# Four transformer layers on one core: another order inside the steps of the second layer, and a split, transposed output projection in the last

## The chip, the cores and the metric

The kernel runs on one core of a Trainium2 chip. The metric is the device time of one execution in microseconds (us), lower is better.

## The reference, cut to what matters

Four layers work one after the other on a residual x of 16 x 256 tokens by 128 features, all in float32. Each normalizes x and adds an attention branch and a feed-forward branch. The second and the last layer are the ones that matter here.

```
# second layer: 16 heads of 64, sequences of 256, sparse causal mask; 8 experts of 256, the best two gate
xn = layernorm(x)
x  = x + attention(xn) @ w_out + sum_e square(relu((xn * gate_e) @ up_e.T)) @ down_e.T
# gate_e = sigmoid(xn @ gate_w.T)[e] where e is among the two largest of sigmoid + expert_bias, else 0

# last layer: 16 heads of 64, causal mask; the linear feed-forward is one 128x128 matrix and a bias
xn = layernorm(x)
x  = x + softmax(q k^T / 8 + mask) v @ Wo + bo + xn @ (int4(kernel) + a @ b) + bias
```

## The kernel before, in words

Every engine has its own program, written out by hand, and the engines meet only at counting semaphores. The second layer (`second_layer`, lines 1119 to 1586) and the last layer (`last_layer`, from line 2052) are built alike. The work is cut into 8 passes of 512 tokens (two sequences), and each pass into 8 pairs of heads: 64 pairs, `N` in the code. A loop over steps `s` runs over the pairs as a software pipeline. In step s, TensorE (PE in the profile) does, in program order:

1. the scores of pair s-1 (L1250 and L1253 in the second layer, L2136 and L2139 in the last), 
2. the weighted values of pair s-3 (L1265, L1269; L2151, L2155),
3. four `turned` units of pair s-2, transposes of the softmax weights (L1278; L2164), with the query projection of pair s between the second and the third (L1230 to L1232; L2116 to L2118), 
4. the key projection of pair s, by the same lines,
5. `output` of pair s-3: the output projection of the pair, summed over the pass in one PSUM bank, `ACC` (L1286; L2172 and L2175),
6. in the second layer: the first up projection of expert (s-2) mod 8 (`up`, L1295 to L1297), `down` of pair s-3 (L1303), and the second up projection,
7. in some steps one more item (below),
8. `values` for step s+1 (L1239 to L1241; L2125 to L2127).

The projections in float32r (fp32r) are three products of a high and a low part: hi x hi, lo x hi, hi x lo; one float32r instruction is one record of the trace. A plain float32 product shows as two records.

The last item of a step in the second layer depends on s mod 8. At 6 it is `turn`, which transposes the normalized rows of the next pass (L1210). At 7 it is `logits`, ahead of the key projection (L1217). At 0 it is `gates_turned` (L1223). At 3, from step 11 on, it is `turned_back` (L1311), which transposes the finished sum of a pass back to rows.

**Two PSUM banks, `RING`, serve all these items in turn.** The list `ITEMS` gives their order. An item may be written when the item two places before it has been read: `ring` in `pe_` waits for it, through `taken`. Who reads what: ScalarE (ACT) copies queries, keys, values and `turn`; VectorE (DVE) multiplies an up projection with its gate (`gated`, L1494) and adds `turned_back` to x (`added`, L1500). In the list before, the two up projections stand side by side and `values` is last.

VectorE's order in a step of the second layer: the four `maxima` of pair s-1 (L1476, L1477; two instructions and their accumulator reads each), the four copies `turned_out` of pair s-2 (L1486) with two reciprocals among them (`sums`, L1481), the first `gated`, then one part of the next pass's normalization (s mod 8 = 4 `moments`, 5 `normed`, 6 `rest` (L1454), 7 `gates`, which is nine dependent instructions, L1460 to L1470), the second `gated`, and `added` at 3. `turned` on TensorE waits for `maxima` of the next pair, because both use the same banks. `rest` waits for ScalarE's two copies of `turn` (L1383, L1384). GpSimd (POOL) scales the weights (L1550) and squares the gated values (L1556), which `down` reads.

In the last layer `output` multiplies in plain float32 with the heads' output as stationary operand: four products of 128 columns per pair (L2175), and once a pass four more with the folded feed-forward matrix (L2172). `ACC` then holds rows, and `added` (L2303) adds it in two halves to x; each half is stored by its own DMA (L2367). ScalarE's `heads_out` (L2215) brings the heads' output from PSUM to SBUF. VectorE's order is that of the second layer without `gated` (maxima L2286 and L2287, copies L2296, reciprocals L2291), GpSimd's only the scaling (L2348).

Of the kernel before, what the change touches and what calls it, by code (L numbers as in the profile page):

```python
# [11 lines left out]
PASSES = B // 2  # L12
# [70 lines left out]
def program(nc, ins, out):  # L83
# [3 lines left out]
    with ctx:  # L87
# [1031 lines left out]
        def second_layer():  # L1119
# [28 lines left out]
            for s in range(-1, N + 4):  # L1148
# [6 lines left out]
                if 0 <= s - 2 < N:  # L1155
                    ITEMS += [("u", 2 * (s - 2)), ("u", 2 * (s - 2) + 1)]
# [30 lines left out]
            ended.update(r_full=r_full, r_taken=r_act, xs_s=xs_s, dv=dv, s_f=s_f, s_mx=s_mx, s_ex=s_ex, s_rc=s_rc, s_nm=s_nm, s_t=s_t, s_te=s_te,  # L1187
# [11 lines left out]
            def pe_(pe):  # L1199
# [120 lines left out]
                for s in range(-1, N + 4):  # L1320
# [107 lines left out]
            def dve_(dve):  # L1428
# [77 lines left out]
                for s in range(-1, N + 4):  # L1506
# [17 lines left out]
                    if 0 < i < PASSES:  # L1524
# [527 lines left out]
        def last_layer():  # L2052
# [14 lines left out]
            ot = [carve(512) for _ in range(2)]  # L2067
# [10 lines left out]
            for s in range(-1, N):  # L2078
                if s >= 0:
                    ITEMS += [("q", s), ("k", s)]  # L2080
                if (s + 2) % PAIRS == 0 and s + 2 < N:
                    ITEMS.append(("t", (s + 2) // PAIRS))
                if s + 1 < N:
                    ITEMS.append(("v", s + 1))
            item = {what: n for n, what in enumerate(ITEMS)}

# [10 lines left out]
            ln_b = sem("l3_biased")  # L2097

            def pe_(pe):
                def ring(kind, n):  # L2100
                    past(pe, r_taken, item[kind, n] - 1)
# [27 lines left out]
                def scores(g):  # L2129
                    past(pe, r_taken, item["k", g] + 1)  # L2130
# [11 lines left out]
                def weighted(g):  # L2142
                    i, j = divmod(g, PAIRS)
                    past(pe, s_te, UNITS * (g + 1))
                    past(pe, r_taken, item["v", i * PAIRS + j // 4 * 4 + 3] + 1)
                    past(pe, s_ot, g)
# [36 lines left out]
                for s in range(-1, N + 3):  # L2183
                    if 0 <= s - 1 < N:
                        scores(s - 1)
                    if 0 <= s - 3:
# [11 lines left out]
                    if 0 <= s - 3:  # L2198
                        output(s - 3)
                    if ("t", (s + 2) // PAIRS) in item and s >= 0 and (s + 2) % PAIRS == 0:  # L2200
                        turn((s + 2) // PAIRS)
                    if s + 1 < N:
                        values(s + 1)

            def act_(act):
# [6 lines left out]
                def heads_out(g):  # L2212
                    past(act, s_pv, g + 1)
                    past(act, o_f, g - 1)
                    act.activation(ot[g % 2], HEADS_OUT[:, :], ACT.Copy).then_inc(s_ot.s, 1)  # L2215
# [17 lines left out]

                turned_out(0)
                for s in range(-1, N + 3):
# [263 lines left out]
```

## Time and profile before

| | us |
|---|---|
| median of 3 runs | 2066.94 (2066.08 to 2068.91) |
| the profiled execution | 2069.05 |
| its span | 2067.2 |
| TensorE busy in the span | 1877.5 (91%) |
| VectorE, ScalarE, GpSimd busy | 1324.3, 1125.2, 869.7 |
| mean granted TensorE clock | 0.959 of full |
| second layer's steps | about 422 to 1154 |
| last layer's steps | about 1576 to 2067 |

Times in the trace count from the span's start. An engine's busy time includes all its instructions that compute; matmuls overlap at their ends, so a step is best measured from one start to the next. The row of an instruction says how long its engine stood idle before it, and for whom, in square brackets; no bracket means that nothing of note was waited for.

### The profile page before, as it was taken

The numbers are of one execution on the slowest core, as the hardware profiler recorded it, in microseconds if no ns is written. First come the engines' busy times: TensorE is split into PE (matmuls) and PEld (weight loads), VectorE is DVE, ScalarE is ACT, GpSimd is POOL, SyncE is SP. The second block draws the span as 40 slices with busy tenths as digits, with TensorE's granted clock in tenths as the row PEclk, the third lists the DMA queues.
The fourth block names the chain that finished last, engine by engine and source line by source line (L and its number), as shares of the span: only waits on it lengthen the run. The fifth ranks groups of instructions, "written<-read, shape, count | busy, mean of one in ns | idle before, by whom it ended". The sixth has DMA issues, their size and how long they took to land.

```text
span 2067.2 us, 40179 instructions
## 1 busy us (share of the span) xinstructions
PE 1877.5 (91%) x13354; PEld 1339.7 (65%) x13354; DVE 1324.3 (64%) x4752; ACT 1125.2 (54%) x3357; POOL 869.7 (42%) x1361
## 2 busy tenths in 40 slices
PE   5787888389999999999999899999998999999999
PEld 2555654266666666666666566666666777777777
DVE  6999973365656565665565566666653666766665
ACT  3444253154545455555555356555555777777776
POOL 4112266545544545454545311111112555555554
PEclk9899699689999999999999899999998999999999
DMA  6000016631010201011010000000000000000000
GB/s 195 22 2 1 2 34 153 130 133 37 7 42 1 42 1 42 6 37 42 1 42 1 1 1 1 1 1 1 1 1 1 7 1 7 7 7 7 6 7 6
DMA packets 74970, 53.62 MB, mean 26 GB/s; under 512 B 7056, under 2 KB 72976, under 8 KB 73872
## 3 DMA queue, kind: packets, MB, share of 16 engines
q1 hardware_dynamic: 69136, 46.73, 8.0%
q0 software_dynamic: 5632, 4.33, 1.5%
q8 instruction: 110, 1.80, 0.4%
q14 instruction: 92, 0.75, 0.1%
HBM read 40.30 MB, written 10.75 MB: 25 GB/s over the span
## 4 chain that ended last, share of the span: by engine, by line
PE 66%; DVE 9%; ACT 3%; issue 3%; POOL 1%; DMA 0%; POOLq 0%; DVEq 0%; ACTq 0%
PE bank L1303 5%; PE bank L1278 5%; PE bank L2164 4%; PE bank L1265 3%; PE bank L2151 3%; PE bank L1253 3%; PE bank L2175 3%; PE bank L1286 3%; PE bank L2139 3%; PE bank L1250 2%; PE bank L2136 2%; PE bank L1676 2%; PE bank L1747 2%; PE bank L1230 1%; PE bank L1297 1%
## 5 line engine op out<-in xcount | busy, mean ns | idle before, releaser
L1550 POOL TENSOR_TENSOR work<-work 128x128 f32<-128x128 f32 (+1 forms) x512 | 243.1, 506 | 248.1 <-DVE work L1481 248.0
L2348 POOL TENSOR_TENSOR work<-work 128x128 f32<-128x128 f32 (+1 forms) x512 | 243.2, 506 | 232.6 <-DVE work L2291 232.6
L1556 POOL TENSOR_TENSOR work<-work 128x512 f32<-128x512 f32 x128 | 133.0, 1040 | 109.5 <-PE bank L1303 61.1
L2296 DVE COPY work<-bank 128x384 f32<-128x384 f32 x256 | 134.5, 548 | 34.4 <-PE bank L2164 33.6
L1486 DVE COPY work<-bank 128x384 f32<-128x384 f32 x256 | 133.9, 547 | 34.4 <-PE bank L1278 34.4
L1379 ACT ACTIVATE work<-bank 128x512 f32<-128x512 f32 x64 | 38.2, 597 | 197.4 <-PE bank L1241 197.4
L1358 ACT ACTIVATE work<-work 128x128 f32<-128x128 f32 x256 | 100.6, 393 | 77.8 <-DVE work L1477 77.8
L2209 ACT ACTIVATE work<-work 128x128 f32<-128x128 f32 x256 | 100.5, 392 | 60.0 <-DVE work L2287 60.0
L2286 DVE CUSTOM_DVE_ANT_0 work<-bank,mask 128x128 f32<-128x128 f32 x256 | 73.5, 287 | 90.8 <-PE bank L2139 90.7
L1494 DVE SCALAR_TENSOR_TENSOR work<-bank,w_f 128x512 f32<-128x512 f32 x96 | 66.3, 690 | 95.3 <-PE bank L1297 95.3
L1359 ACT ACTIVATE work<-work 128x256 f32<-128x256 f32 x256 | 126.8, 495 | 0.0
L2210 ACT ACTIVATE work<-work 128x256 f32<-128x256 f32 x256 | 126.7, 495 | 0.0
L1303 PE MATMUL bank<-work,w_l 128*128 128x512 f32 x256 | 120.3, 592 | 0.0
L1476 DVE CUSTOM_DVE_ANT_0 work<-bank,mask 128x128 f32<-128x128 f32 x256 | 73.5, 287 | 72.2 <-PE bank L1253 71.8
L1278 PE MATMUL bank<-w_const,work 128*128 128x128 f32 x768 | 109.5, 278 | 0.4
L2164 PE MATMUL bank<-w_const,work 128*128 128x128 f32 x768 | 108.1, 277 | 0.0
L2287 DVE CUSTOM_DVE_ANT_0 work<-bank,mask 128x256 f32<-128x256 f32 x256 | 107.5, 420 | 0.0
L1477 DVE CUSTOM_DVE_ANT_0 work<-bank,mask 128x256 f32<-128x256 f32 x256 | 107.4, 420 | 0.0
L2031 POOL TENSOR_TENSOR work<-work,minus_half 128x4 f32<-128x4 f32 x8 | 8.5, 1060 | 227.7 <-DVEq L1893 227.7
L1278 PEld LDWEIGHTS bank<-w_const,work 128*128 128x128 f32 x768 | 86.8, 141 | 22.1 <-issue 13.6
L1295 PE MATMUL bank<-l_xn_hi,l_up_hi 128*128 128x512 f32 x128 | 99.7, 779 | 0.1
L2164 PEld LDWEIGHTS bank<-w_const,work 128*128 128x128 f32 x768 | 86.8, 141 | 20.1 <-issue 11.4
(389 smaller groups left out, 5436.3 us busy)
## 6 DMA issues: line engine op xcount, KB each, us to landing
w_f<-gates SPq DMA_DIRECT2D x48, 256.0 KB, 6.1
w_const<-gates SPq DMA_DIRECT2D x16, 256.0 KB, 5.7
w_l<-in_l SPq DMA_DIRECT2D x1, 3210.5 KB, 15.1
w_l<-in_l SPq DMA_DIRECT2D x2, 1540.0 KB, 7.5
w_f<-in_f SPq DMA_DIRECT2D x1, 3072.0 KB, 14.0
x_sb<-in_x SPq DMA_DIRECT2D x4, 512.0 KB, 5.8
normed_rows<-work SPq DMA_DIRECT2D x1, 2048.0 KB, 9.4
even_experts<-x_sb SPq DMA_DIRECT2D x8, 256.0 KB, 3.6
```

The costliest lines, as they stand in the source:

```text
L1278: mm = pe.transpose(PS[u][:, to * 128:(to + 1) * 128], pr[g % 2][u][:, c * 128:(c + 1) * 128], ident)
L1303: mm = pe.matmul(ACC[:, :], L["down"][:, (2 * e + c) * D:(2 * e + c + 1) * D], h2[c], start=False, stop=(e == PAIRS - 1 and c == 1), skip_ ...
L1359: act.activation(w[:, Q1], w[:, Q1], ACT.Exp, scale=-1.0, bias=nmx[:, g % 2, u, 1:2], accum_out=sm[:, g % 2, u, 1:2]).then_inc(s_ex.s, 1)
L1477: dve.tensor_tensor_reduce(w[:, Q1], PS[u][:, Q1], mask1[:, Q1], -1.0, BIG, ALU.add, ALU.min, nmx[:, g % 2, u, 1:2]).then_inc(s_mx.s, 1)
L1486: dve.tensor_copy(pt[u], PS[u][:, 0:384]).then_inc(s_te.s, 1)
L1550: ins_ = pool.tensor_tensor(w, w, spread(rc[:, g % 2, u, q:q + 1], w.shape[1]), ALU.mult)
L1556: pool.tensor_tensor(h2[u % 2], hs[u % 2], hs[u % 2], ALU.mult).then_inc(f_q.s, 1)
L2164: mm = pe.transpose(PS[u][:, to * 128:(to + 1) * 128], pr[g % 2][u][:, c * 128:(c + 1) * 128], ident)
L2210: act.activation(w[:, Q1], w[:, Q1], ACT.Exp, scale=-1.0, bias=nmx[:, g % 2, u, 1:2], accum_out=sm[:, g % 2, u, 1:2]).then_inc(s_ex.s, 1)
L2287: dve.tensor_tensor_reduce(w[:, Q1], PS[u][:, Q1], mask3[:, Q1], -1.0, BIG, ALU.add, ALU.min, nmx[:, g % 2, u, 1:2]).then_inc(s_mx.s, 1)
L2296: dve.tensor_copy(pt[u], PS[u][:, 0:384]).then_inc(s_te.s, 1)
L2348: ins_ = pool.tensor_tensor(w, w, spread(rc[:, g % 2, u, q:q + 1], w.shape[1]), ALU.mult)
```

## The change

In the second layer, TensorE's step ends differently. The item of step 7 (turn, gates_turned or turned_back) now stands right behind the first up projection, `down` behind it, then `values`, and the second up projection ends the step. `ITEMS` follows that order. On VectorE `added` moves ahead of the second `gated`, and `rest` and `gates` move behind it; `moments` and `normed` stay.

In the last layer the output projection is turned over and split: the weights are the stationary operand, the heads' output of 512 tokens is the moving one, and each is a high and a low float32r part. `ACC` now holds features by tokens, as in the second layer. So each pass is copied out by ScalarE, transposed back on TensorE as a ring item, and added in one piece; one step is added at the end. VectorE makes the low part of the heads' output (`heads_rest`) in every step. The parts of the weights are made once at the start.

```diff
 # second layer, ITEMS
-                    ITEMS += [("u", 2 * (s - 2)), ("u", 2 * (s - 2) + 1)]
+                    ITEMS.append(("u", 2 * (s - 2)))
...
                 if s + 1 < N:
                     ITEMS.append(("v", s + 1))
+                if 0 <= s - 2 < N:
+                    ITEMS.append(("u", 2 * (s - 2) + 1))
...
 # second layer, TensorE
                         up(2 * (s - 2))
-                    if 0 <= s - 3 < N:
-                        down(s - 3)
-                    if 0 <= s - 2 < N:
-                        up(2 * (s - 2) + 1)
...
                         turned_back((s - 11) // PAIRS)
+                    if 0 <= s - 3 < N:
+                        down(s - 3)
                     if s + 1 < N:
                         values(s + 1)
+                    if 0 <= s - 2 < N:
+                        up(2 * (s - 2) + 1)
...
 # second layer, VectorE
+                    if s >= 11 and (s - 11) % PAIRS == 0:
+                        added((s - 11) // PAIRS)
+                    if 0 <= s - 2 < N:
+                        gated(2 * (s - 2) + 1)
+                    if 0 < i < PASSES:
                         if at == 2:
                             rest(i)
                         if at == 3:
                             gates(i)
-                    if 0 <= s - 2 < N:
-                        gated(2 * (s - 2) + 1)
-                    if s >= 11 and (s - 11) % PAIRS == 0:
-                        added((s - 11) // PAIRS)
...
 # last layer, TensorE
                 def output(g):
                     i, j = divmod(g, PAIRS)
                     if j == 0:
-                        past(pe, o_e, 2 * i)
-                        for t in range(4):
-                            pe.matmul(ACC[:, t * 128:(t + 1) * 128], xnT[:, t * 128:(t + 1) * 128], w_eff, start=(t == 0), stop=False, skip_group_check=True)
-                    past(pe, s_ot, g + 1)
+                        past(pe, y_s, i)
+                        pe.matmul(ACC[:, :], w_eff, xnT, start=True, stop=False, skip_group_check=True)
+                    if g == 0:
+                        past(pe, w_lo, 1)
+                    past(pe, s_or, g + 1)
+                    ws = slice(j * 128, (j + 1) * 128)
+                    pe.matmul(ACC[:, :], wout_hi[:, ws], ot_hi[g % 2], start=False, stop=False, skip_group_check=True)
+                    pe.matmul(ACC[:, :], wout_hi[:, ws], ot_lo[g % 2], start=False, stop=False, skip_group_check=True)
+                    pe.matmul(ACC[:, :], wout_lo[:, ws], ot_hi[g % 2], start=False, stop=(j == PAIRS - 1), skip_group_check=True).then_inc(o_f.s, 1)
+
+                def turned_back(i):
+                    to = ring("b", i)
+                    past(pe, y_s, i + 1)
                     for t in range(4):
-                        mm = pe.matmul(ACC[:, t * 128:(t + 1) * 128], ot[g % 2][:, t * 128:(t + 1) * 128], L["wout"][:, j * 128:(j + 1) * 128],
-                                       start=False, stop=(j == PAIRS - 1), skip_group_check=True)
-                    mm.then_inc(o_f.s, 1)
+                        mm = pe.transpose(to[:, t * 128:(t + 1) * 128], yT[:, t * 128:(t + 1) * 128], ident)
+                    mm.then_inc(r_full.s, 1)
...
 # last layer, ScalarE: once at the start, and once a pass at s = 10, 18, ...
+                def sum_out(i):
+                    past(act, o_f, PAIRS * (i + 1))
+                    act.activation(yT, ACC[:, :], ACT.Copy).then_inc(y_s.s, 1)
...
+                act.activation(wout_hi, L["wout"], ACT.Copy).then_inc(w_hi.s, 1)
...
 # last layer, VectorE
+                def heads_rest(g):
+                    past(dve, s_ot, g + 1)
+                    past(dve, o_f, g - 1)
+                    dve.tensor_tensor(ot_lo[g % 2], HEADS_OUT[:, :], ot_hi[g % 2].bitcast(F32), ALU.subtract).then_inc(s_or.s, 1)
...
+                dve.tensor_tensor(wout_lo, L["wout"], wout_hi.bitcast(F32), ALU.subtract).then_inc(w_lo.s, 1)
...
-                        for u in (1, 2, 3):
+                        turned_out(s - 2, 1)
+                    if 0 <= s - 3 < N:
+                        heads_rest(s - 3)
+                    if 0 <= s - 2 < N:
+                        for u in (2, 3):
                             turned_out(s - 2, u)
```

## Rows read from the trace of the kernel before

**Rows 1.** Windows of the two layers: window, length, each engine's busy time, PEclk, DMA.

```profile
415.00:1140.00 725.00, 695.40 (x4218) 476.99 (x4218) 438.81 (x1705) 378.21 (x1314) 378.66 (x644) 0.98 0.12 31
1575.00:2067.00 492.00, 485.03 (x3988) 384.86 (x3986) 324.37 (x1522) 369.00 (x1293) 257.40 (x526) 1.00 0.02 6
```

**Rows 2.** TensorE's waits in the second layer: total us, times, longest.

```profile
PE bank L1239 <- DVE work L1494: 24.6, 21, 2.5
```

**Rows 3.** Timeline, start and length: first scores of steps 30 to 36.

```profile
743.35 0.49 PE L1250 MATMUL bank<-work 64*128 64x128 f32 x4
...
757.31 0.80 PE L1250 MATMUL bank<-work 64*128 64x128 f32 x4
...
770.03 0.49 PE L1250 MATMUL bank<-work 64*128 64x128 f32 x4
...
781.88 0.49 PE L1250 MATMUL bank<-work 64*128 64x128 f32 x4
...
792.38 0.49 PE L1250 MATMUL bank<-work 64*128 64x128 f32 x4
...
802.87 0.49 PE L1250 MATMUL bank<-work 64*128 64x128 f32 x4
...
814.42 0.49 PE L1250 MATMUL bank<-work 64*128 64x128 f32 x4
```

**Rows 4.** Timeline of all engines, end of step 30: turn, then rest on VectorE.

```profile
753.06 0.60 PE L1210 MATMUL bank<-w_const,work 128*128 128x128 f32 x4
...
754.81 0.69 DVE L1454 TENSOR_TENSOR l_xn_lo<-work,l_xn_hi 128x512 fp32r<-128x512 f32 x1 [3.27 <-ACT l_xn_hi L1384]
```

**Rows 5.** Windows behind the first pass's wait and behind the fourth's.

```profile
480.00:484.40 4.40, 2.71 (x23) 1.86 (x25) 2.16 (x9) 1.09 (x3) 1.04 (x1) 1.00 0.00 0
756.10:760.20 4.10, 4.04 (x21) 2.57 (x21) 1.20 (x9) 1.12 (x4) 1.04 (x1) 0.58 0.00 0
```

**Rows 6.** Timeline, end of step 34 and start of step 35, an undisturbed step.

```profile
802.28 0.69 DVE L1494 SCALAR_TENSOR_TENSOR work<-bank,w_f 128x512 f32<-128x512 f32 x1 [1.72 <-PE bank L1297]
...
802.55 0.40 PE L1241 MATMUL bank<-l_wv_hi,l_xn_lo 128*128 128x512 f32 x1
...
803.83 0.29 DVE L1476 CUSTOM_DVE_ANT_0 work<-bank,mask 128x128 f32<-128x128 f32 x1 [0.85 <-PE bank L1253]
...
806.78 0.40 PE L1231 MATMUL bank<-l_xn_lo,l_qk_hi 128*128 128x512 f32 x1
```

**Rows 7.** Timeline: gates of the first pass; gates in step 31 and what followed.

```profile
413.84 0.18 DVE L1460 TENSOR_SCALAR work<-work 128x32 f32<-128x32 f32 x1 [1.47 <-ACT work L1389]
...
417.07 1.88 DVE L982 TENSOR_TENSOR x_sb<-x_sb,w_f 128x1664 f32<-128x1664 f32 x1
...
767.64 0.17 DVE L1460 TENSOR_SCALAR work<-work 128x32 f32<-128x32 f32 x1
...
771.70 0.69 DVE L1494 SCALAR_TENSOR_TENSOR work<-bank,w_f 128x512 f32<-128x512 f32 x1
...
774.25 0.40 PE L1231 MATMUL bank<-l_xn_lo,l_qk_hi 128*128 128x512 f32 x1
```

**Rows 8.** Chain of waits in the last layer: start, length, line, records.

```profile
1801.32 0.44 PE bank L2108 x4
...
1815.45 0.23 PE bank L2118
1815.68 0.89 PE bank L2175 x8
```

**Rows 9.** VectorE's timeline in the same step of the last layer.

```profile
1814.69 1.02 DVE L2296 COPY work<-bank 128x384 f32<-128x384 f32 x2 [0.27 <-PE bank L2164]
1816.03 0.18 DVE L2291 RECIPROCAL work<-work 128x4 f32<-128x4 f32 x1 [0.32 <-ACT work L2210]
```

**Rows 10.** Timeline of all engines, end of the kernel.

```profile
2062.09 0.60 ACT L2215 ACTIVATE work<-bank 128x512 f32<-128x512 f32 x1 [3.44 <-PE bank L2155]
...
2063.93 0.75 DVE L2303 TENSOR_TENSOR x_sb<-x_sb,bank 128x256 f32<-128x256 f32 x2 [3.47 <-PE bank L2175]
```

More of the change, by code:

```diff
@@ L2066, in last_layer @@
             pt = [carve(384) for _ in range(UNITS)]
-            ot = [carve(512) for _ in range(2)]
+            ot_at = top[0]
+            carve(4, 512)
+            ot_hi, ot_lo = ([rounded(f"l3_{part}_{p}", "work", ot_at + (2 * n + p) * 512, 512) for p in range(2)]
+                            for n, part in enumerate(("heads_hi", "heads_lo")))
+            yT = carve(512)
+            wout_hi, wout_lo = rounded("l3_wout_hi", "w_l2", 0, WIDE), rounded("l3_wout_lo", "w_f0", WIDE, WIDE)
             nmx, sm, rc = carve(2, UNITS, 2), carve(2, UNITS, 2), carve(2, UNITS, 2)
@@ L2077, in last_layer @@
             ITEMS = [("t", 0)]
-            for s in range(-1, N):
-                if s >= 0:
+            for s in range(-1, N + 4):
+                if 0 <= s < N:
                     ITEMS += [("q", s), ("k", s)]
-                if (s + 2) % PAIRS == 0 and s + 2 < N:
+                if s >= 0 and (s + 2) % PAIRS == 0 and s + 2 < N:
                     ITEMS.append(("t", (s + 2) // PAIRS))
+                if s >= 11 and (s - 11) % PAIRS == 0:
+                    ITEMS.append(("b", (s - 11) // PAIRS))
                 if s + 1 < N:
@@ L2085, in last_layer @@
             item = {what: n for n, what in enumerate(ITEMS)}
+            by_act = [kind != "b" for kind, _ in ITEMS]
+            act_rank = [sum(by_act[:n]) for n in range(len(ITEMS))]
             def bank_of(kind, n):
@@ L2097, in last_layer, with taken @@
             ln_b = sem("l3_biased")
+            s_or, y_s = ended["f_d"].next(), ended["y_s"].next()
+            w_hi, w_lo = Count(g_bv, 3, 1), Count(g_sct, 1, 1)
+            def taken(eng, kind, n):
+                if kind == "b":
+                    past(eng, o_e, n + 1)
+                else:
+                    past(eng, r_taken, act_rank[item[kind, n]] + 1)
             def pe_(pe):
                 def ring(kind, n):
-                    past(pe, r_taken, item[kind, n] - 1)
+                    m = item[kind, n]
+                    if m >= 2:
+                        taken(pe, *ITEMS[m - 2])
                     return bank_of(kind, n)
@@ L2129, in scores @@
                 def scores(g):
-                    past(pe, r_taken, item["k", g] + 1)
+                    taken(pe, "k", g)
                     for p in range(2):
@@ L2182, in pe_ @@
                 pe.wait_ge(weights_rest, 3)
-                for s in range(-1, N + 3):
+                for s in range(-1, N + 4):
                     if 0 <= s - 1 < N:
                         scores(s - 1)
-                    if 0 <= s - 3:
+                    if 0 <= s - 3 < N:
                         weighted(s - 3)
@@ L2197, in pe_ @@
                         project("k", s)
-                    if 0 <= s - 3:
+                    if 0 <= s - 3 < N:
                         output(s - 3)
-                    if ("t", (s + 2) // PAIRS) in item and s >= 0 and (s + 2) % PAIRS == 0:
+                    if s >= 0 and (s + 2) % PAIRS == 0 and s + 2 < N:
                         turn((s + 2) // PAIRS)
+                    if s >= 11 and (s - 11) % PAIRS == 0:
+                        turned_back((s - 11) // PAIRS)
                     if s + 1 < N:
@@ L2248, in act_ @@
                         projected("k", s)
-                    if ("t", (s + 2) // PAIRS) in item and s >= 0 and (s + 2) % PAIRS == 0:
+                    if s >= 0 and (s + 2) % PAIRS == 0 and s + 2 < N:
                         turned_out((s + 2) // PAIRS)
+                    if s >= 10 and (s - 10) % PAIRS == 0:
+                        sum_out((s - 10) // PAIRS)
                     if s + 1 < N:
@@ L2278, in rest @@
                 def rest(i):
-                    past(dve, r_taken, item["t", i] + 1)
+                    taken(dve, "t", i)
                     dve.tensor_tensor(x_lo[i % 2], xnT, x_hi[i % 2].bitcast(F32), ALU.subtract).then_inc(xs_s.s, 1)
@@ L2308, in dve_ @@
                 rest(0)
-                for s in range(-1, N + 3):
+                past(dve, w_hi, 1)
+                dve.tensor_tensor(wout_lo, L["wout"], wout_hi.bitcast(F32), ALU.subtract).then_inc(w_lo.s, 1)
+                for s in range(-1, N + 4):
                     i, at = divmod(s + 4, PAIRS)
@@ L2329, in dve_ @@
                             rest(i)
-                    if s >= 3 and (s - 3) % PAIRS == PAIRS - 1:
-                        added((s - 3) // PAIRS)
+                    if s >= 11 and (s - 11) % PAIRS == 0:
+                        added((s - 11) // PAIRS)
             def pool_(pool):
@@ L2352, in pool_ @@
                 bias(0)
-                for s in range(-1, N + 3):
+                for s in range(-1, N + 4):
                     i, at = divmod(s + 4, PAIRS)
@@ L2364, in sp_ @@
             def sp_(sp):
-                for n in range(2 * PASSES):
-                    past(sp, o_e, n + 1)
-                    sp.dma_start(out_v[:, 2 * n:2 * n + 2, :], x_sb[:, 2 * n:2 * n + 2, :]).then_inc(stored, 16)
+                for i in range(PASSES):
+                    past(sp, o_e, i + 1)
+                    for n in (4 * i, 4 * i + 2):
+                        sp.dma_start(out_v[:, n:n + 2, :], x_sb[:, n:n + 2, :]).then_inc(stored, 16)
             pe_prog.append(pe_)
```

21 lines of the change are left out of this document (10 added, 11 removed).

## The prediction

> **What bounds the kernel now.** I read the page first: TensorE is busy for 91% of the span and no other engine for more than 64%. The windows of the two layers that change come next [rows 1]. In the second layer TensorE works 695.4 of 725 us, in the last 485.0 of 492, and the clock is full there. So in both layers a gain comes from less work on TensorE or from one of its few waits. The waits of TensorE in the second layer name one line: `values` (L1239) stands for 24.6 us in 21 places, 2.5 us at most, until VectorE has done a `gated` [rows 2]. The starts of the scores show where [rows 3]. An ordinary step is 792.38 - 781.88 = 10.50 us. Steps 30, 31, 32 and 35 (6, 7, 0 and 3 modulo 8) take 13.96, 12.72, 11.85 and 11.55. This pattern comes seven times.
>
> The timeline of step 30 tells why. `turn` starts at 753.06, ScalarE copies its result, and `rest` on VectorE can start only at 754.81, having waited 3.27 us [rows 4]. The second `gated` stands behind `rest` in VectorE's program, and `values` needs the bank that this `gated` reads. So TensorE's own transposes come back to it as a wait of 2.5 us. Behind the wait the clock is low: 0.58 of full over 4.10 us, against 1.00 behind the same wait of the first pass [rows 5]. A share of 0.58 is mostly the lower level of 1.2 GHz, and 4.10 x (1 - 0.58) = 1.7 us are lost by it, in steps 30 and 31.
>
> **Second layer, what goes.** In the new list the item of step 7 has the key projection two places before it, `values` has the first up projection, and the second up projection has the item. After `turn` come `down` (two float32 products as wide as the whole output projection, 0.89 each by [rows 8]) and `values` before the second up projection, over 2 us, and `turn` is read by two copies of ScalarE of 0.60 each (size as in [rows 10]). So steps 30 and 31 lose the wait and the slow clock: 2.5 + 1.7 = 4.2 us. In step 35 `turned_back` adds 11.55 - 10.50 = 1.05 us now, while four such transposes on the path of the last layer are worth 0.44 [rows 8]. `added` is done before the second up projection needs its bank, so 0.6 us go.
>
> **Second layer, what is late next.** In an ordinary step nothing changes. `gated` of the second up projection starts at 802.28 and the three float32r products of `values` took 3 x 0.23 = 0.70 us (size as L2118 in [rows 8]). With the two exchanged `gated` runs from 802.98 to 803.67, and `maxima` starts at 803.83, when the scores are there [rows 6]. That leaves 0.16 us. In step 30 `rest`, 0.69 us, now stands between them. `maxima` comes 0.5 to 0.6 us late.
>
> How much lateness of `maxima` TensorE bears is read from step 32. There `maxima` started at 771.70 + 0.6 = 772.3, which is 2.27 after the scores at 770.03, where 803.83 - 802.87 = 0.96 is usual: 1.3 late. The second query product stood at 774.25 - 770.03 = 4.22 after the scores, where 806.78 - 802.87 = 3.91 is usual: 0.3 late [rows 3, 6, 7]. So TensorE bears 1.0 us, `rest` costs nothing, and each further us of lateness is a us of waiting.
>
> `gates` is more than that. It now runs behind the second `gated`, directly ahead of `maxima` of step 32. Nine instructions took 771.70 - 767.64 = 4.06 us in step 31 and 417.07 - 413.84 = 3.23 in the first pass, where GpSimd was idle [rows 7]. Behind them on VectorE wait `maxima`, the copies and the reciprocals. For the first of these TensorE waits at its first `turned`, and ScalarE with all exponentials, from which heads, query and key copies hang. With 4.06 `maxima` starts 0.8 + 4.06 = 4.9 after the scores, 3.9 late, and TensorE stands 2.9 us. With 3.23 it is 2.1 us. I take 2.6, since GpSimd's square of the second up projection runs beside it at the new place too. ScalarE stays 1 us later than TensorE; `gates_turned` now needs the bank of the key copy directly behind the first up projection. This costs between 0 and 1.0; I take 0.4, as the up projection covers half. The clock costs between 0 and 1.7, as in [rows 5]. I take 0.9, since a part is hidden in the waits for ScalarE. The item itself is a transpose of one tile, 0.25 at most by the 0.44 for four. Step 32 is then 10.5 + 0.25 + 2.6 + 0.4 + 0.9 = 14.65, against 11.85: 2.8 us more.
>
> The Trainium skill, page "SBUF — State Buffer", section "SBUF: two separate sides", says that a VectorE instruction with two SBUF inputs and a GpSimd instruction that reads SBUF lock each other out for a whole instruction. By that rule only one square of about 1 us, begun some 0.5 us before, stands against `gates` at its new place, so it would take 3.7 us and TensorE would wait 2.5. The two durations in [rows 7] agree with such a lock.
>
> Per pass: -4.2 - 0.6 + 2.8 = -2.0 us. Seven times this is -14.0. In the first pass the clock had not fallen [rows 5], so 1.7 of it was never there: **second layer -12.3 us**. The ends are 0 + 1.7 + 7 x (-4.2 - 0.6 + 4.5) = about 0 and 7 x (-4.2 - 0.6 + 1.0) + 1.7 = -25. The DMAs of the gates start as late as before, since `gates_turned` comes some 2 us earlier in its step and the step 3 us later.
>
> **Last layer, per step.** The output projection of a pair is 0.89 us on the chain, and one float32r product of 128x512 is 0.23 [rows 8]. Three of them are 0.70: -0.19 us, and 64 pairs give -12.2. The four products with the feed-forward matrix become one of 512 columns, the same work, 0. New on TensorE are four transposes a pass, 0.44 each time [rows 8], seven of them inside: +3.1.
>
> The Trainium skill, page "FP8 and Floating Point Precision", section "TensorE Precision Notes", says that a true float32 product is four passes of the array. By that rule three passes in place of four would save 0.89 / 4 = 0.22 a pair, 14.2 in all.
>
> New on VectorE is `heads_rest`, 128x512 with one input in PSUM, 0.69 as `gated` [rows 6], between the second and the third copy. VectorE stands 0.27 before the third copy and 0.32 before the second reciprocal [rows 9], so 0.59 of it are covered and the reciprocal is at most 0.1 late. That feeds GpSimd's weights of the third and fourth unit, which TensorE wants in the next step. Cost 0; the lower end is a gain of 0 for the whole layer's steps, if the cover fails in part. ScalarE's `sum_out` (0.60) comes once a pass, where it waits for `values`. `wout_hi` and `wout_lo`, two instructions of 128x1024, run at the start and are wanted three steps later: 0. The waits of TensorE for `heads_rest` in place of ScalarE's copy are over a us before `output`.
>
> **Last layer, the end.** The last steps have no projections, and VectorE's copies are on the chain. `heads_rest` stands between them twice: +1.2. After the last ScalarE copy at 2062.09 to 2062.69 the sum was added from 2063.93 on, 1.24 later [rows 10]. Now come `heads_rest` 0.69, three products about 0.9, `sum_out` 0.60, four transposes 0.44 to 0.6, and about 0.05 at each of four hand-overs: 2.9, which is 1.7 more. The store of the first half no longer starts before the second half is added: +0.3. Together **+3.2**, between 1.5 and 4.5. The last layer: -12.2 + 3.1 + 3.2 = **-5.9 us**.
>
> **The sum.** -12.3 - 5.9 = -18.2. The profiled execution took 2069.05 (span 2067.2), so 2050.85. The median of the runs is 2066.94, 2.11 below it, which gives **2048.7**.
>
> **Rivals.**
> *The clock stays high.* If it does not fall behind the new wait of step 32, 0.9 x 7 = 6.3 go too: 2042.4. For it: in the first pass 2.5 us of waiting left the clock at 1.00, and the new wait is broken by the transposes of the first unit. Against it: the fourth pass [rows 5].
> *The wait only moves.* If TensorE stands 2.9, all of ScalarE's 1.0 and the whole 1.7 of clock are paid, step 32 is 4.5 longer, and the second layer gives about 0: 2066.94 - 5.9 = 2061. For it: `gates` needs 4.06 with GpSimd busy. Against it: waits for ScalarE and slow products overlap.
> *VectorE bounds the last layer, slower.* If `heads_rest` shifts the third and fourth copy so that its 0.69 stands on TensorE's path in each step, a step is 0.69 - 0.19 = 0.5 longer, 64 x 0.5 = +32. With +3.1 + 3.2 - 12.3 this is +26: 2093. It decides from the point where VectorE's idle time of 0.59 and the time until TensorE's next weighted values, in the next step, are used up. Against it: VectorE is busy for 324 of 492 us [rows 1], and 64 x 0.69 = 44 more are 75%.
> *The new order does nothing to the wait*, if `values` still waits for a `gated` behind `rest`. The program order excludes this.
>
> **Chances.** Forecast (gain of 9 to 24) 0.62; clock high 0.14; the wait only moves 0.14; slower by VectorE 0.05; other mishaps of either sign 0.05. Runs of this kernel differ by some 0.1%, so a change under 0.2% (4.1 us) can't be told from none. Faster by more than that 0.90, within it 0.04, slower 0.06. The range reaches from a high clock with short `gates` to most of the second rival: 2037 to 2060.
>
> **What would show it.** L1239 loses its waits for L1494. Steps 6, 7, 3 modulo 8 take about 10.95, 11.3 and 10.95; step 0 about 14.6, with TensorE standing at L1278's successor for VectorE's maxima behind `gates`. Steps of the last layer take 7.2 in place of 7.4. The forecast is wrong if step 0 stays at 12, or if a line of the last layer's transposes or weighted values begins to wait for VectorE in each step.

## The result, and the profile after

The changed kernel takes **2047.95 us** (median of four runs, 2046.20 to 2049.94). The kernel before took 2067.93 on the same chip (2066.08 to 2071.29). The ratio is 0.9902, with an interval of 0.9885 to 0.9919. The forecast was 2048.7, with 2037 to 2060 as its range.

The profiled execution took 2049.94 us with a span of 2048.1. The stages are those of [rows 1], but with both edges in the idle time beside the layers, and the two short windows are explained below. The columns are those of [rows 1].

```profile
410.00:1120.00 710.00, 682.04 (x4211) 471.88 (x4212) 437.64 (x1716) 377.23 (x1310) 378.86 (x636) 0.98 0.12 33
1560.00:2048.00 488.00, 476.07 (x3648) 361.21 (x3646) 357.07 (x1578) 373.06 (x1300) 257.56 (x526) 0.99 0.02 6
764.50:769.00 4.50, 2.33 (x28) 1.50 (x25) 4.22 (x16) 0.28 (x1) 1.04 (x1) 1.00 0.02 4
502.00:507.00 5.00, 5.00 (x19) 3.71 (x18) 2.53 (x8) 3.78 (x13) 3.42 (x8) 0.70 0.00 0
```

TensorE's waits in the second layer are the counterpart of [rows 2]. The line `values` had 24.6 us there. It is gone, and `turned` (L1280) waits for `maxima` (L1479) instead, once a pass. A short wait of `gates_turned` for ScalarE's copy is new too.

```profile
PE bank L1280 <- DVE work L1479: 15.2, 7, 2.2
...
PE bank L1225 <- ACT work L1375: 1.5, 5, 0.3
```

The first scores of steps 30 to 36 are the counterpart of [rows 3].

```profile
741.33 0.49 PE L1252 MATMUL bank<-work 64*128 64x128 f32 x4
...
752.26 0.49 PE L1252 MATMUL bank<-work 64*128 64x128 f32 x4
...
763.63 0.49 PE L1252 MATMUL bank<-work 64*128 64x128 f32 x4
...
777.15 0.49 PE L1252 MATMUL bank<-work 64*128 64x128 f32 x4
...
787.65 0.49 PE L1252 MATMUL bank<-work 64*128 64x128 f32 x4
...
798.13 0.49 PE L1252 MATMUL bank<-work 64*128 64x128 f32 x4
...
809.06 0.49 PE L1252 MATMUL bank<-work 64*128 64x128 f32 x4
```

From these starts and those of the other passes, a step measures as follows (s modulo 8; us; the mean over the passes where they differ):

| | before | after | forecast |
|---|---|---|---|
| second layer, ordinary step | 10.50 | 10.50 | same |
| step 6 | 13.90 | 10.93 | 10.95 |
| step 7 | 12.55 | 11.37 | 11.3 |
| step 0 | 11.84 | 13.81 (five of 13.53, one of 14.39, one of 14.63) | 14.65 |
| step 3 | 11.55 | 10.93 | 10.95 |
| **step 1's scores (the first) to step 63's** | 699.37 | 679.68: **-19.7** | -12.3 |
| last layer, ordinary step | 7.40 | 7.21 | 7.21 |
| step 6 / step 3 | 7.85 / 8.29 | 7.65 / 8.52 | |
| **step 1's scores (the first) to step 63's** | 467.97 | 459.42: **-8.6** | -9.1 |
| **step 63's scores to the span's end** | 23.08 | 28.9: **+5.8** | +3.2 |

Two parts outside these steps also moved. All that comes ahead of the second layer's first scores, where both kernels are the same, took 426.98 us after 422.62 (+4.4). In the traces of the experiments the same stretch took 422.46 to 435.64, so this is a spread between executions and chips. The stretch from step 63 of the second layer to the first scores of the last took 453.12 after 454.16 (-1.0). The sum is -19.7 - 8.6 + 5.8 + 4.4 - 1.0 = -19.1, the difference of the two spans. This is why the effects below are read from the lengths of steps, and the times only support them.

Step 32 starts at 763.63. These are VectorE, GpSimd and TensorE in it, from the timeline of all engines:

```profile
763.63 0.49 PE L1252 MATMUL bank<-work 64*128 64x128 f32 x4
763.74 0.69 DVE L1496 SCALAR_TENSOR_TENSOR work<-bank,w_f 128x512 f32<-128x512 f32 x1 [2.41 <-PE bank L1299]
...
764.35 0.17 DVE L1462 TENSOR_SCALAR work<-work 128x32 f32<-128x32 f32 x1
...
764.51 1.04 POOL L1559 TENSOR_TENSOR work<-work 128x512 f32<-128x512 f32 x1 [1.00 <-DVE work L1496]
...
764.94 0.66 DVE L1464 TENSOR_TENSOR work<-work,w_l 128x32 f32<-128x32 f32 x1
...
768.04 0.29 DVE L1478 CUSTOM_DVE_ANT_0 work<-bank,mask 128x128 f32<-128x128 f32 x1
...
768.83 1.08 PE L1280 MATMUL bank<-w_const,work 128*128 128x128 f32 x6 [2.17 <-DVE work L1479]
...
769.98 0.40 PE L1233 MATMUL bank<-l_xn_lo,l_qk_hi 128*128 128x512 f32 x1
```

`gates` runs from 764.35 to 768.04, which is 3.69 us. GpSimd's square stands beside it only once, and L1464 takes 0.66 there, where the same line takes 0.19 with GpSimd idle (the timeline of VectorE further below). TensorE waits 2.17 us. The lock-out that the Trainium skill tells of ("SBUF — State Buffer", section "SBUF: two separate sides") thus fits the rows. The estimates by it in the prediction, 3.7 for `gates` and 2.5 for the wait, lay nearer than the 2.6 that I took. They too are over the 2.17 of this row. The section on the prediction takes the same wait by the prediction's own measure.

The end of the kernel is the counterpart of [rows 10]:

```profile
2038.37 0.60 ACT L2248 ACTIVATE l_heads_hi<-bank 128x512 fp32r<-128x512 f32 x1 [4.04 <-PE bank L2178]
2039.00 0.69 DVE L2341 TENSOR_TENSOR l_heads_lo<-bank,l_heads_hi 128x512 fp32r<-128x512 f32 x1 [2.25 <-ACT l_heads_hi L2248]
...
2039.74 0.50 PE L2199 MATMUL bank<-l_heads_hi,l_wout_hi 128*128 128x512 f32 x1 [1.42 <-DVE l_heads_lo L2341]
...
2040.73 0.60 ACT L2269 ACTIVATE work<-bank 128x512 f32<-128x512 f32 x1 [1.77 <-PE bank L2201]
...
2041.47 1.09 PE L2207 MATMUL bank<-w_const,work 128*128 128x128 f32 x4 [0.78 <-ACT work L2269]
2042.60 0.69 DVE L2347 TENSOR_TENSOR x_sb<-x_sb,bank 128x512 f32<-128x512 f32 x1 [2.91 <-PE bank L2207]
2043.32 0.89 SPq L2417 DMA_DIRECT2D out_x<-x_sb  x2
```

From the end of the last copy of the heads to the end of the last add it is 2043.29 - 2038.97 = 4.32 us, against 1.99 before. The four transposes take 1.09 here.

### The profile page after: what moved, and what is told of

Same layout as the page of the kernel before. It is cut to its first block, busy times and chain, and to the rows that moved or that the text cites. A ratio compares the mean times of both kernels' runs of the same rounds, so it can differ in the third digit from the quotient of the medians.

```text
span 2048.1 us, 39644 instructions
## 1 busy us (share of the span) xinstructions
PE 1867.9 (91%) x13018; PEld 1317.7 (64%) x13018; DVE 1357.2 (66%) x4809; ACT 1130.1 (55%) x3366; POOL 873.2 (43%) x1361
## 4 chain that ended last, share of the span: by engine, by line
PE 63%; DVE 10%; ACT 4%; issue 3%; POOL 2%; DMA 0%; POOLq 0%; DVEq 0%; ACTq 0%
PE bank L1305 5%; PE bank L2187 4%; PE bank L1280 4%; PE bank L2174 3%; PE bank L1267 3%; PE bank L2162 3%; PE bank L1288 2%; PE bank L1255 2%; PE bank L2159 2%; PE bank L1252 2%; PE bank L1679 2%; PE bank L1750 2%; PE bank L2139 1%; PE bank L2140 1%; PE bank L2141 1%
## 5 line engine op out<-in xcount | busy, mean ns | idle before, releaser
L1280 PE MATMUL bank<-w_const,work 128*128 128x128 f32 x768 | 110.9, 281 | 15.4 <-DVE work L1479 15.2
L2326 DVE CUSTOM_DVE_ANT_0 work<-bank,mask 128x128 f32<-128x128 f32 x256 | 73.3, 287 | 74.3 <-PE bank L2162 74.2
L1280 PEld LDWEIGHTS bank<-w_const,work 128*128 128x128 f32 x768 | 88.3, 142 | 37.1 <-issue 28.8
L1479 DVE CUSTOM_DVE_ANT_0 work<-bank,mask 128x256 f32<-128x256 f32 x256 | 107.6, 420 | 0.0
L441 ACT ACTIVATE w_l<-bank 76x512 f32<-76x512 f32 x128 | 71.0, 590 | 51.0 <-PE bank L811 50.7
L323 POOL TENSOR_TENSOR w_l<-qk,w_const 128x304 f32<-128x304 f32 x16 | 12.0, 752 | 187.1 <-ACT qk L427 187.0
```

Source lines behind the costliest of these rows:

```text
L1280: mm = pe.transpose(PS[u][:, to * 128:(to + 1) * 128], pr[g % 2][u][:, c * 128:(c + 1) * 128], ident)
L1479: dve.tensor_tensor_reduce(w[:, Q1], PS[u][:, Q1], mask1[:, Q1], -1.0, BIG, ALU.add, ALU.min, nmx[:, g % 2, u, 1:2]).then_inc(s_mx.s, 1)
```

## The experiments

Each ran beside the kernel before on its chip. The first four shared one chip (before: 2069.02), as did the next four (2076.5) and the last two (2068.88). Ratios are against these. The times expected in experiments 5 to 8 were reckoned from kernels on a chip with 2068 to 2069, so there the steps and the ratios decide, not the microseconds.

**1. The second layer alone.** The changed kernel with the last layer of before, whole.

> The second layer of the changed kernel with the last layer of the kernel before: only the order of the second layer is changed. Theory (the two parts add up and the order is worth the most): the steps of the second layer sum to 19.7 us less, as in the trace after, so the time is about 17 to 20 us under the kernel before, near 2048 to 2050. Rival (part of the gain of the second layer in that trace is the state of the run, and the last layer gives more than its steps show): 10 to 13 us under it, near 2056. Steps 0 modulo 8 should take 13.5 us, or 14.4 to 14.6 where the clock falls, and the others 10.5 to 11.4.

Measured: 2052.45 us (2049.02 to 2053.23), ratio 0.9915 (0.9882 to 0.9947). The second layer is that of the changed kernel: 680.06 us between the same scores, and step 0 takes 14.70, 14.62 and five times 13.53. The last layer takes 7.40 a step and 23.1 at the end. So the last layer's -8.6 and +5.8 do not come from the second layer's edit. The gain of 16.6 us falls just short of the 17 to 20 expected and far from the rival's 10 to 13. The steps gave 19.3.

**2. The last layer alone.** The kernel before with the last layer of after, whole.

> The second layer of the kernel before with the last layer of the changed kernel. Theory: steps 7.21 in place of 7.40, steps with turned_back 8.52 in place of 8.29, and an end that is 3.5 to 6 us longer; together 2.5 to 5 us under the kernel before. Rival (the end is longer only by the two heads_rest and the added hand-overs, as predicted, 3.2 us, and the 2 us beyond that in the trace after are one slow store): 5 to 6 us under it. If the store again lands 3.9 us after its issue, it is not chance.

Measured: 2068.11 (2060.34 to 2070.07), ratio 0.9987 (0.9971 to 1.0004), not told from 1. The steps are 7.21, 8.52 and 7.65, together 459.54. The end takes 26.52. The wait of `values` in the second layer stands as before:

```profile
PE bank L1239 <- DVE work L1494: 24.6, 21, 2.5
```

The last layer's edit by its own rows gives 459.54 - 467.97 = -8.4 and 26.52 - 23.08 = +3.4, in all -5.0 us. That lies inside the interval, but the 0.9 us between the medians can't confirm it. The gain of the whole change is thus nearly all in the second layer.

**3. `gates` back ahead of the second `gated`,** `rest` stays behind it.

```diff
+                    if 0 < i < PASSES and at == 3:
+                        gates(i)
                     if 0 <= s - 2 < N:
                         gated(2 * (s - 2) + 1)
-                    if 0 < i < PASSES:
-                        if at == 2:
-                            rest(i)
-                        if at == 3:
-                            gates(i)
+                    if 0 < i < PASSES and at == 2:
+                        rest(i)
```

> The changed kernel with gates ahead of the second gated on VectorE, rest still behind it. Theory (the wait that is left in step 0 is the 3.2 to 4.1 us of gates that stand directly ahead of maxima): VectorE is idle for about 2.4 us between the two gated, gates fills that gap, so maxima comes only about 0.8 to 1.6 us late, of which TensorE bears 1.0; step 0 falls from 13.5 to 10.8 to 11.5, and seven passes give 14 to 19 us: 2029 to 2034. Rival (what TensorE waits for in step 0 is ScalarE's late exponentials and copies, or the bank of gates_turned): the second gated comes later too, the key projection waits for it, and the step stays over 12.5; under 7 us gained, 2041 or more.

Measured: **2026.66** (2023.89 to 2027.20), ratio 0.9794 (0.9763 to 0.9825). Step 0 takes 11.39 in all seven passes, the others as after. Its wait of 2.17 us is gone. This beats both kernels. VectorE's timeline at the same place shows why:

```profile
748.49 0.19 DVE L1464 TENSOR_TENSOR work<-work,w_l 128x32 f32<-128x32 f32 x1
...
749.17 1.26 DVE L1466 TENSOR_TENSOR w_l<-w_l,w_const 128x256 f32<-128x256 f32 x1
...
750.28 0.49 PE L1252 MATMUL bank<-work 64*128 64x128 f32 x4
...
751.95 0.69 DVE L1496 SCALAR_TENSOR_TENSOR work<-bank,w_f 128x512 f32<-128x512 f32 x1
752.56 0.28 DVE L1478 CUSTOM_DVE_ANT_0 work<-bank,mask 128x128 f32<-128x128 f32 x1
```

`gates` starts at 747.90 and runs to 751.95, which is 4.05, longer than at the later place (L1466 takes 1.26 here, beside GpSimd's square, and 0.42 in the changed kernel). But more than half of it lies in time in which VectorE would wait for the second up projection, 2.41 us in the changed kernel. `maxima` starts 2.28 us after the scores (752.56 - 750.28), where the changed kernel has 4.41 (768.04 - 763.63). TensorE bears the first but for 0.3 us (the second query product starts 4.23 after the scores, where 3.91 is usual), and not the second.

**4. The kernel before with only `rest` behind the second `gated`.** TensorE's order, `gates` and the last layer are as before.

```diff
-                        if at == 2:
-                            rest(i)
                         if at == 3:
                             gates(i)
                     if 0 <= s - 2 < N:
                         gated(2 * (s - 2) + 1)
+                    if 0 < i < PASSES and at == 2:
+                        rest(i)
```

> The kernel before with one edit: rest moves behind the second gated on VectorE; TensorE's order and the ring stay. Theory (the wait of 2.5 us was made by VectorE's order alone, rest ahead of gated, and not by the place of values on TensorE): values waits at turn as little as at turned_back, 0.3 us; step 6 falls from 13.9 to 11.3, step 7 to 11.4, step 0 stays 11.85 and step 3 11.55; seven passes give 22 to 27 us: 2040 to 2045, more than the whole change. Rival (TensorE's order was needed, because values stands directly behind turn and needs the bank that the second gated reads): under 8 us gained.

Measured: 2043.54 (2041.02 to 2045.11), ratio 0.9871 (0.9839 to 0.9904). Step 6 takes 11.54, step 7 11.38, steps 0 and 3 as before. Of the wait there is left:

```profile
PE bank L1239 <- DVE work L1494: 9.6, 21, 0.7
```

The time is the one expected, 2040 to 2045. The waits that are left are longer than the expected 0.3, so step 6 is 0.2 over its 11.3. One line of VectorE's program, moved in the old kernel, gives as much as the whole change.

**5. Both `rest` and `gates` ahead again,** TensorE's new order stays.

```diff
-                    if 0 <= s - 2 < N:
-                        gated(2 * (s - 2) + 1)
                     if 0 < i < PASSES:
                         if at == 2:
                             rest(i)
                         if at == 3:
                             gates(i)
+                    if 0 <= s - 2 < N:
+                        gated(2 * (s - 2) + 1)
```

> The changed kernel with rest and gates both back ahead of the second gated on VectorE; TensorE's order and added stay as changed. Theory (either half of the change takes the 2.5 us wait away: with TensorE's order the bank of values no longer hangs on the gated behind rest): step 6 stays 10.93 and step 7 11.4, step 0 is 11.4 as with gates alone ahead; within 2 us of that kernel, 2025 to 2029. Rival (VectorE's order was needed too): rest waits for ScalarE until the second up projection is done and step 6 goes back over 12, 14 us or more slower than that kernel.

Measured: 2030.74 (2027.66 to 2038.77), ratio 0.9793 (0.9761 to 0.9825). The steps are 10.93, 11.37, 11.38 and 10.93, those of experiment 3. So with TensorE's new order the place of `rest` does not matter, and that of `gates` costs 2.1 us a pass.

**6. VectorE's new order alone:** the kernel before with `rest` and `gates` behind the second `gated`, the reverse of experiment 5's edit.

> The kernel before with rest and gates behind the second gated; TensorE's order, the ring and added stay. Theory (gates behind the second gated is what makes step 0 long, whatever TensorE's order): step 6 11.54, step 7 11.38, step 0 longer than its 11.85 of before: the second gated comes 0.7 us earlier here, so maxima is 2.8 us late and TensorE stands for 1.6 to 1.9; 12.9 to 13.3, so that the kernel is 7 to 10 us slower than with rest alone behind: 2050 to 2054. Rival (the new place of the second up projection at the end makes the wait): step 0 stays under 12.2 and the time is 2044 to 2046.

Measured: 2059.42 (2058.45 to 2063.81), ratio 0.9922 (0.9901 to 0.9943). Step 6 takes 11.54, step 7 11.38, step 0 13.27 to 13.30, all as expected. Its new wait:

```profile
PE bank L1278 <- DVE work L1477: 10.3, 7, 1.5
PE bank L1239 <- DVE work L1494: 9.6, 21, 0.7
```

`gates` at the late place costs here too, 13.3 - 11.85 = 1.45 a pass. Seven times this is 10 us, about the distance of the ratios, 0.9922 against the 0.9871 of experiment 4.

**7. `heads_rest`'s subtraction twice.** The first one goes to a spare tile that nothing reads.

```diff
                     past(dve, o_f, g - 1)
+                    dve.tensor_tensor(spare[g % 2], HEADS_OUT[:, :], ot_hi[g % 2].bitcast(F32), ALU.subtract)
                     dve.tensor_tensor(ot_lo[g % 2], HEADS_OUT[:, :], ot_hi[g % 2].bitcast(F32), ALU.subtract).then_inc(s_or.s, 1)
```

> The changed kernel with the subtraction of heads_rest done twice in every step (the first result is not used). Theory (VectorE in the last layer has about 1.5 us left in a step, and only the short idle times before the third copy and the second reciprocal are used by one heads_rest): the doubled one shifts the third and fourth copy by 0.6 more, the reciprocal by 0.5, and nobody on TensorE waits for it: steps stay 7.21 to 7.3, the kernel is 0 to 6 us slower. Rival (VectorE is at its limit with one, as in the slower case that was forecast): each step is 0.6 longer, 64 x 0.6 = 38 us slower, about 2086.

Measured: 2069.04 (2060.20 to 2072.92), ratio 0.9959 (0.9943 to 0.9975), against 0.9902 with one. A step takes 7.47, 0.26 more than 7.21. Both expectations miss: the subtraction is neither covered nor paid in full. TensorE waits at `output` itself, in 54 of the 64 places. First TensorE's weight loader in the last layer's waits, then the timeline of one such step:

```profile
PEld bank L2200 <- DVE l_heads_lo L2343: 25.5, 54, 1.6
```

```profile
1739.01 0.68 DVE L2342 TENSOR_TENSOR work<-bank,l_heads_hi 128x512 f32<-128x512 f32 x1
1739.61 0.68 DVE L2343 TENSOR_TENSOR l_heads_lo<-bank,l_heads_hi 128x512 fp32r<-128x512 f32 x1
...
1740.34 0.50 PE L2200 MATMUL bank<-l_heads_hi,l_wout_hi 128*128 128x512 f32 x1
```

The second starts 0.60 after the first, and 0.26 come through. The changed kernel has about 0.34 us to spare there. Its own timeline agrees: `heads_rest` ends at 1734.82 and `output` starts at 1735.32.

```profile
1734.14 0.68 DVE L2341 TENSOR_TENSOR l_heads_lo<-bank,l_heads_hi 128x512 fp32r<-128x512 f32 x1
...
1735.32 0.39 PE L2199 MATMUL bank<-l_heads_hi,l_wout_hi 128*128 128x512 f32 x1
1735.55 0.39 PE L2200 MATMUL bank<-l_heads_lo,l_wout_hi 128*128 128x512 f32 x1
1735.78 0.39 PE L2201 MATMUL bank<-l_heads_hi,l_wout_lo 128*128 128x512 f32 x1
```

**8. The last layer turned over, but not split.** One plain float32 product of 128x512 stands for the three float32r ones. `heads_rest`, `wout_hi` and `wout_lo` are gone.

```diff
-                    pe.matmul(ACC[:, :], wout_hi[:, ws], ot_hi[g % 2], start=False, stop=False, skip_group_check=True)
-                    pe.matmul(ACC[:, :], wout_hi[:, ws], ot_lo[g % 2], start=False, stop=False, skip_group_check=True)
-                    pe.matmul(ACC[:, :], wout_lo[:, ws], ot_hi[g % 2], start=False, stop=(j == PAIRS - 1), skip_group_check=True).then_inc(o_f.s, 1)
+                    pe.matmul(ACC[:, :], L["wout"][:, ws], ot[g % 2], start=False, stop=(j == PAIRS - 1), skip_group_check=True).then_inc(o_f.s, 1)
```

> The changed kernel whose last layer keeps the turned orientation of the output projection but not the split: one plain float32 product of 512 columns a pair, no heads_rest and no split weights. Theory (the gain of a step is float32r's three passes for four, 0.19 us, and turning alone gives next to nothing): steps 7.36 to 7.40, steps with turned_back 8.65 to 8.70; last layer 5 to 8 us longer than in the changed kernel after the savings of heads_rest in the end, 2052 to 2057. Rival (four short products with four loads of the stationary operand were the cost, not the number of passes): steps 7.21 to 7.25 and the time within 2 us of the changed kernel.

Measured: 2059.69 (two runs, 2057.56 and 2061.82), ratio 0.9925 (0.9896 to 0.9954). A step takes 7.39, step 3 8.69, step 6 7.83. The split is worth 7.39 - 7.21 = 0.18 a pair, and turning the product over alone is worth 0.01.

**9. Experiment 3 with `gates_turned` behind `down` on TensorE.**

```diff
-                    if s > 0 and s % PAIRS == 0 and s < N:
-                        gates_turned(s // PAIRS)
                     if s >= 0 and (s + 2) % PAIRS == 0 and s + 2 < N:
                         turn((s + 2) // PAIRS)
                     if s >= 11 and (s - 11) % PAIRS == 0:
                         turned_back((s - 11) // PAIRS)
                     if 0 <= s - 3 < N:
                         down(s - 3)
+                    if s > 0 and s % PAIRS == 0 and s < N:
+                        gates_turned(s // PAIRS)
```

> The changed kernel with gates ahead of the second gated on VectorE, and gates_turned behind down on TensorE. Theory (what is left in step 0 is the wait of gates_turned for the bank of the late key copy, 0.3 us, which down's 1.7 us would cover): the wait is gone, step 0 falls from 11.39 to 11.1 or somewhat under, 2 us in all, and the gates' DMAs start 1.7 us later without harm, as 12 us are left to their first use. Rival (the gates then come late, or a float32 transpose between down and values costs as much as the wait did): step 0 stays 11.3 to 11.4.

Measured: 2026.70 (2023.50 to 2028.93), ratio 0.9788 (0.9759 to 0.9817). Step 0 takes 10.92 in place of 11.39, and the wait for ScalarE's copy is gone from it. That is 3.3 us by the steps, more than the 2 expected. The times don't show it, since experiment 3 has 2026.66. This trace took 428.08 us to the first scores, where that of experiment 3 took 422.46, and its last store landed late.

**10. The changed kernel again,** for the end and the clock.

> The changed kernel once more, beside the one before and the one with both edits on the same chip. Theory: 1.0% under the kernel before; the last store lands 1.9 us after its issue, so that the end, from the last step's first scores, is 26.6 to 27 us and not the 28.9 of the first trace; the seven steps 0 take 13.5 us where the clock stays high and 14.4 to 14.7 where it falls. Rival (the late store belongs to the change): 28.9 us again.

Measured: 2045.30 (2043.12 to 2048.98), ratio 0.9884 (0.9854 to 0.9915). Step 0 takes 14.57 once and 13.53 six times, as expected. The end does not: it takes 28.5 and not 26.6 to 27, and its last store again lands late, 3.6 us after its issue. Here the rival was right.

## Why the prediction was right, and where it was not

The time came out 0.8 us from the forecast, and the mechanism of each layer is the one foretold. The closeness of the number is partly luck: the second layer gave 7.4 us more, the last 3.1 less, and the parts outside the steps took 3.4 more, which is mostly the spread of the stretch ahead of them.

- **The wait of `values` goes.** Right: L1239's 24.6 us are gone, and steps 6, 7 and 3 are within 0.1 of their forecast. The prediction gave TensorE's new order as the reason. Experiment 5 shows that this suffices. Experiment 4 shows what it did not say: VectorE's order alone nearly suffices too, and the two do not add. For step 3 no run moved TensorE's order and `added` apart, so which of them gives its 0.6 us is not shown.
- **The clock comes back in steps 6 and 7.** Right, and a little more than forecast: the two steps lose 2.97 + 1.18 = 4.15 in the mean of all seven passes, 29.1 in all. The forecast was 7 x 4.2 - 1.7 = 27.7.
- **Step 0, the term that was mis-sized.** Forecast 14.65, measured 13.81. The wait was nearly right. `gates` took 3.69, between the 3.23 and 4.06 of [rows 7]. `maxima` started 4.41 after the scores, where 0.96 is usual, 3.45 late. By the measure of the prediction, the second query product, TensorE was 769.98 - 763.63 - 3.91 = 2.44 behind, against the 2.6 forecast. So it bore the 1.0 that was read from step 32 of before. (The 2.17 in the brackets is the part of it ahead of the first `turned`.) The rest of the step, the item and its bank, took 13.53 - 10.49 - 2.44 = 0.60, for 0.25 + 0.4. The mis-sized term is the clock: 0.9 was taken for each pass, but it fell behind two of seven waits only. The two steps are 1.1 and 0.9 longer than the rest, 2.0 in all or 0.3 a pass. The windows in the result show both kinds: 1.00 through step 32's wait, and 0.70 behind step 8's. The rows of step 8's second query product show the same price:

```profile
500.72 1.10 PE L1280 MATMUL bank<-w_const,work 128*128 128x128 f32 x6 [2.17 <-DVE work L1479]
...
502.05 0.63 PE L1233 MATMUL bank<-l_xn_lo,l_qk_hi 128*128 128x512 f32 x1
```

  It is 0.63, where this product takes 0.40 in step 32 and at full clock in the kernel before [rows 7]. The seven passes give 7 x (14.65 - 13.81) = 5.9 of the 7.4. The rest is the 1.4 of the point above and 0.1 of step 3.
- **The item of step 0.** In experiment 9, with the wait for ScalarE gone too, step 0 takes 0.43 more than an ordinary step. Of this 0.32 is there by the second query product, because of `gates`. So 0.1 is left for the item at that place, against the 0.25 allowed.
- **The last layer's split.** Right: 0.18 to 0.19 a pair (experiments 2 and 8). The Trainium skill's four passes of a float32 product ("FP8 and Floating Point Precision", section "TensorE Precision Notes") would have given 0.22. The step shows a little less than this estimate.
- **Four transposes a pass.** Forecast 3.1 for seven. Step 3 rose by 0.23 while the ordinary step fell by 0.19, so it is 0.42 each, 2.9 in all. Right.
- **`heads_rest` at no cost.** Right, but with less cover than was said. "Over a us before `output`" is wrong: it is 0.34 to 0.5 us (experiment 7). The rival "VectorE bounds the last layer" was therefore nearer than its 0.05. The place was another than it named, namely `output`, and its price 0.26 a step and not 0.5.
- **The end, the second term that was mis-sized.** Forecast +3.2, measured +5.8. `weighted` of the last two pairs cost 0.6 each, as forecast (1.2). The chain from the last copy to the add's end grew by 2.33, where 1.7 was taken: the transposes took 1.09 for the 0.6 allowed. The store cost another 2.3, from the add's end to the span's end 4.8 after 2.5, where 0.3 was taken. Of this 2.0 is the second store, which landed 3.9 us after its issue and not 1.9. That is no term of the prediction. The 0.3 for the store that starts later is what remains. Where the last store landed in time (experiments 2 and 3), the end is 3.4 and 3.9 longer than before.
- **The rivals.** "The clock stays high" was nearly right as a mechanism, for five of seven passes, and 4.3 of its 6.3 us were had. "The wait only moves" is ruled out by the steps: 13.5 and not 16.4. The slower case did not come.

## What to carry to other kernels

Where two engines take turns at a ring of banks, ask for each short job on the helper engine whether it stands ahead of the work that frees a bank, and in which idle time it falls. The same 4 us of `gates` cost TensorE 0.3 us a pass ahead of `gated` (experiment 3) and 2.1 more behind it. When a change reorders two engines at once, try each half alone: here each half removes the wait, and one of them brings a cost that the other does not need. The best kernel takes TensorE's new order and leaves VectorE's `gates` where they were (2026.7 against 2048).

## What was not expected of the hardware

**The clock behind equal waits.** In the changed kernel seven waits of 2.17 us with the same work ahead of them left the clock alone in five cases, and in six of seven when the same kernel ran again. Which ones fell is not pure chance. Five traces have this wait (the two of the changed kernel and experiments 1, 7 and 8), and in all five the first pass fell: step 8 takes 14.49 to 14.70. One more fell in three of them, step 24 or step 16, and none later. In the old order it is the other way round: behind 2.5 us of waiting the clock fell in six of seven passes, and the one spared is the first, in the trace of the kernel before and in experiment 2 (steps 6 and 7 take 25.1 there and 26.6 to 26.7 in the other passes). The seven waits of 1.5 us in experiment 6 left the clock at full. So neither the length of a wait nor the pass alone tells what follows, and the prediction's hint from the first pass pointed the wrong way for that pass. What decides is open. Such a term is best kept as a range, and counted over all passes of more than one trace.

**Stores that land late in pairs.** Each pass's results go out by two DMAs of 128 KB issued 0.42 us apart. In the kernel before all landed 1.9 us after issue. In the changed kernel the last two landed 2.1 and 3.9 after it. First before, then after, the view of the store's line in the last microseconds: the two issues, and the time from issue to landing:

```profile
L2367 SPq DMA_DIRECT2D out_x<-x_sb x2: 372/421/470, 2064.4 to 2064.8; - x2
...
DMA to landing us min/median/max: 1.9/1.9/1.9
```

```profile
L2417 SPq DMA_DIRECT2D out_x<-x_sb x2: 372/422/472, 2043.3 to 2043.7; - x2
...
DMA to landing us min/median/max: 2.1/3.0/3.9
```

The size and the spacing are the same. Such a pair was seen in every trace with the new last layer (the two of the changed kernel and experiments 2, 3, 5 and 7 to 9): in one or two of the eight pairs, in experiment 7 in four. Its second store landed 2.9 to 4.0 us after issue. No trace with the old layer has one (before, experiments 1, 4 and 6). The places repeat: the third pair is late in all but experiment 8. The last pair was hit in both traces of the changed kernel and in experiments 5, 7 and 9. In the former two and in experiments 5 and 9 the end took 28.1 to 28.9, where experiments 2 and 3, with the last pair spared, have 26.52 and 26.93. Against experiment 3 it cost 1.2 to 2.0 us. Why the new layer brings it out is open. No run tested it.
